# A local-attention layer on one Trainium2 core: SiLU as x times (1 + tanh(x/2)), with the product on VectorE

## What is computed

```python
def _L3_ffn_ref(x, ln_gamma, ln_beta, fc1_q, fc1_scales, fc1_bias, fc2_q, fc2_scales, fc2_bias):
    residual = x
    h = (x - mu) * rsqrt(var + EPS) * ln_gamma + ln_beta      # 8 x 512 tokens of 256
    w1 = _dequant(fc1_q, fc1_scales, G)                       # 256 x 1024
    y = hf @ w1 + fc1_bias
    y = jax.nn.silu(y)                                        # 4096 x 1024
    w2 = _dequant(fc2_q, fc2_scales, G)                       # 1024 x 256
    z = y @ w2 + fc2_bias
    return residual + 0.5 * z.reshape(residual.shape)
```

## Time and profile before

| what | value |
|---|---|
| time, median of 3 runs (lowest, highest) | 3257.53 us (3250.82, 3258.21) |
| the profiled execution | 3265.37 us, span 3263.7 us |
| TensorE busy | 2919.4 us, 89% of the span |
| VectorE busy | 1855.6 us, 57% |
| ScalarE busy | 1379.5 us, 42% |
| GpSimd busy | 327.3 us, 10% |
| layer L3's loop, one pass of seven | 88.67 us |

### The profile page before, as it was taken

One profiled execution on the slowest core, in us unless ns is written; L12 is line 12 of the kernel. 1 busy time (PEld: TensorE's weight loads), 2 busy tenths in 40 slices (PEclk: granted clock), 3 DMA queues, 4 the chain that ended last, 5 costly groups with the idle time before them and its releaser, 6 DMA issues.

```text
span 3263.7 us, 50711 instructions
## 1 busy us (share of the span) xinstructions
PE 2919.4 (89%) x14374; PEld 1828.7 (56%) x14407; DVE 1855.6 (57%) x4470; ACT 1379.5 (42%) x1993; POOL 327.3 (10%) x353
## 2 busy tenths in 40 slices
PE   5999999999989888888789989999997798888888
PEld 3455545554544444444357767766664466666666
DVE  5656665666547777777646666652223555444442
ACT  1544454445425555554454554433232333333333
POOL 0000000000000000000211121121112211111110
PEclk7999999999878999999999999999998899999999
DMA  6433543254122121212230110132211433333340
GB/s 207 138 103 85 162 138 106 81 162 138 55 72 63 57 66 59 63 61 66 76 139 32 51 45 32 45 112 84 86 61 55 123 82 65 91 91 92 78 89 17
DMA packets 144299, 279.77 MB, mean 86 GB/s; under 512 B 22384, under 2 KB 80113, under 8 KB 134161
## 3 DMA queue, kind: packets, MB, share of 16 engines
q1 hardware_dynamic: 131760, 244.90, 26.1%
q0 software_dynamic: 10464, 28.59, 3.1%
q10 hardware_dynamic: 2016, 5.58, 0.5%
HBM read 179.31 MB, written 99.68 MB: 85 GB/s over the span
## 4 chain that ended last, share of the span: by engine, by line
PE 74%; DVE 9%; issue 5%; ACT 4%; DMA 4%; another core or an unknown queue 1%; SPq 1%; DVEq 0%; POOL 0%; ACTq 0%; POOLq 0%
PE bank_u L559 6%; PE pair L599 5%; PE pair L543 5%; PE pair L700 4%; PE pair L1984 4%; PE bank L2426 3%; PE bank L488 3%; DVE nmax L870 3%; PE pair L2883 3%; PE bank_m L2847 3%; PE pair L744 3%; PE bank L2847 3%; PE bank L520 2%; PE pair L499 2%; PE pair L1406 2%
## 5 line engine op out<-in xcount | busy, mean ns | idle before, releaser
L776 ACT ACTIVATE probs<-pair 128x1024 f32<-128x1024 f32 x512 | 501.2, 1020 | 220.2 <-PE pair L543 219.1
L870 DVE TENSOR_REDUCE nmax<-bank 128x1 f32<-128x512 f32 x664 | 442.2, 686 | 210.6 <-PE bank L520 147.8
L870 DVE TENSOR_REDUCE nmax<-bank_m 128x1 f32<-128x512 f32 x360 | 246.7, 685 | 114.5 <-PE bank_m L520 67.6
L559 PE MATMUL bank_u<-probs,vext 128*32 128x512 f32 x2048 | 294.0, 648 | 0.6 <-ACT uraw L763 0.5
L520 PE MATMUL bank<-k_a,q_a 96*128 96x512 f32 x336 | 173.6, 551 | 24.1 <-DMA k_a<-parts_dram 20.6
L543 PE MATMUL pair<-q_a,k_a 98*128 98x512 f32 x512 | 172.6, 444 | 17.1 <-ACT probs L776 11.8
L2019 ACT ACTIVATE probs<-pair 128x896 f32<-128x896 f32 x128 | 115.8, 918 | 131.1 <-PE pair L1906 78.1
L2116 DVE CUSTOM_DVE_ANT_0 bank<-bank,mask_q 128x128 f32<-128x128 f32 (+1 forms) x320 | 118.6, 416 | 80.1 <-PE bank L1888 73.1
L543 PEld LDWEIGHTS pair<-q_a,k_a 98*128 98x128 f32 x512 | 89.2, 199 | 112.5 <-ACT probs L776 65.3
L1379 PE MATMUL bank<-k,q 62*128 62x512 f32 x302 | 115.2, 485 | 26.7 <-DVE nmax L870 26.7
L1984 PE MATMUL pair<-fc,hid 128*128 128x256 f32 x512 | 131.2, 382 | 6.0 <-ACT probs L2019 6.0
(11 more groups left out here) (422 smaller groups left out, 5946.2 us busy)
## 6 DMA issues: line engine op xcount, KB each, us to landing
parts_dram<-parts SPq DMA_DIRECT2D x64, 512.0 KB, 2.8
q_a<-parts_dram SPq DMA_DIRECT2D x31, 512.0 KB, 5.3
k_a<-parts_dram SPq DMA_DIRECT2D x31, 512.0 KB, 7.2
q<-parts_dram SPq DMA_DIRECT2D x97, 128.0 KB, 2.6
xs<-xres SPq DMA_DIRECT2D x24, 512.0 KB, 3.0
xl<-xs SPq DMA_DIRECT2D x24, 512.0 KB, 3.9
x_in<-xg SPq DMA_DIRECT2D x74, 128.0 KB, 2.1
yg_dram<-y_out POOLq DMA_DIRECT2D x72, 128.0 KB, 2.0
```

What stands on the lines that cost most here:

```text
L559: ins = nc.tensor.matmul(bank_u[32 * h:32 * h + 32, :], vext[:, kt, kv(g, h), :], probs[:, kt % 2, h * SEQ:(h + 1) * SEQ], start=(kt == 0) ...
L776: nc.scalar.activation(probs[:, kt % 2, hp * 2 * SEQ:hp * 2 * SEQ + n], st.tile(l, name)[:, 0:n], ACT.Exp).then_inc(st.free["act"].sem, 1)
L870: nc.vector.tensor_reduce(nmax[:, g % 2, qt, h:h + 1], sc.tile(l, name)[:], AX, ALU.max, negate=True).then_inc(sc.free["dve"].sem, 1)
```

## The change

SiLU(y) = y sigmoid(y) = (y / 2) (1 + tanh(y / 2)). ScalarE now writes tanh((h + b)/2) into a new tile `gate3` (one tile for all eight, with the bias halved in `half_b`), then h + b into `hid3[:, i, :]` by Identity, which hands the PSUM bank back. VectorE multiplies: `hid3 = (gate3 + 1) * hid3`. The factor 1/2 goes into `fc2`, which was scaled by 0.5 and is scaled by 0.25 now. A new signal `hid_ready` counts the products: ScalarE's tanh of tile i waits for the product of tile i - 1, since that reads `gate3`, and TensorE's output matmuls wait for all eight. On VectorE product 0 stands ahead of group 3's first maxima, 1 behind two of them, 2 ahead of the fifth and sixth, 3 ahead of the last two, and 4 to 7 in a row behind the splits.

```diff
@@ dve_setup3
-                nc.vector.tensor_scalar(fc2[:], fc2[:], 0.5, None, ALU.mult).then_inc(dve_set3, 1)
+                nc.vector.tensor_scalar(fc2[:], fc2[:], 0.25, None, ALU.mult).then_inc(dve_set3, 1)
+                nc.vector.tensor_scalar(half_b[:], fc1_b[:], 0.5, None, ALU.mult).then_inc(dve_set3, 1)
@@ pe3
-                pe.wait_ge(*done(sc, l, it, ("H", 7)))
+                pe.wait_ge(*hid_ready.at(l, it, 8))
@@ act3
             def hidden(i):
                 act.wait_ge(*sc.filled(l, it, ("H", i)))
-                nc.scalar.activation(hid3[:, i, :], sc.tile(l, ("H", i))[:], ACT.Silu,
+                act.wait_ge(*hid_ready.at(l, it, i))
+                nc.scalar.activation(gate3[:], sc.tile(l, ("H", i))[:], ACT.Tanh, bias=half_b[:, i:i + 1], scale=0.5)
+                nc.scalar.activation(hid3[:, i, :], sc.tile(l, ("H", i))[:], ACT.Identity,
                                      bias=fc1_b[:, i:i + 1]).then_inc(sc.free["act"].sem, 1)
@@ dve3
+            def hidden(first, last):
+                for i in range(first, last):
+                    dve.wait_ge(*done(sc, l, it, ("H", i)))
+                    nc.vector.scalar_tensor_tensor(hid3[:, i, :], gate3[:], 1.0, hid3[:, i, :], ALU.add, ALU.mult)\
+                      .then_inc(hid_ready.sem, 1)
@@ dve3, the order of the back part
             if back:
-                maxima(3, 0, 4)
+                hidden(0, 1)
+                maxima(3, 0, 2)
+                hidden(1, 2)
+                maxima(3, 2, 4)
@@
             if back:
-                maxima(3, 4, 8)
+                hidden(2, 3)
+                maxima(3, 4, 6)
+                hidden(3, 4)
+                maxima(3, 6, 8)
                 dve_normalise_heads(dve, l, it, step, 0)
@@
+            if back:
+                hidden(4, 8)
             if front:
                 dve.wait_ge(*rstd3_ready.at(l, it, 1))
```

More of the change, by code:

```diff
@@ L1803, in build @@
         fc1_b = sb("fc1_b", [P, 8], F32, l3)
+        half_b = sb("half_b", [P, 8], F32, l3)
+        gate3 = sb("gate3", [P, SEQ], F32, l3)
         hn = sb("hn", [P, TT, DIM], F32, l3)
@@ L1827, in build @@
         rstd3_ready = sig("rstd3_ready", [0, 0, 0, (1, 0)], "gpsimd")
+        hid_ready = sig("hid_ready", [0, 0, 0, (0, 8)], "vector")
         hn_ready = sig("hn_ready", [0, 0, 0, (TT, 0)], "vector")
@@ L1847, in dve_setup3 @@
             elif c == 9:
-                nc.vector.tensor_scalar(fc2[:], fc2[:], 0.5, None, ALU.mult).then_inc(dve_set3, 1)
+                nc.vector.tensor_scalar(fc2[:], fc2[:], 0.25, None, ALU.mult).then_inc(dve_set3, 1)
+                nc.vector.tensor_scalar(half_b[:], fc1_b[:], 0.5, None, ALU.mult).then_inc(dve_set3, 1)
             elif c == 10:
-                dve.wait_ge(dve_set3, 10)
+                dve.wait_ge(dve_set3, 11)
                 flat = fc2[:, :, :].rearrange("p k n -> p (k n)")
@@ L3068, in _ @@
                     act_blocks(act, it)
-            act.wait_ge(dve_set3, 12)
+            act.wait_ge(dve_set3, 13)
             act3(act, PRE3, 0, step)
@@ L3157, in _ @@
                 pe.wait_ge(*free.at(PRE3, 0))
-            pe.wait_ge(dve_set3, 12)
+            pe.wait_ge(dve_set3, 13)
             pe.wait_ge(pool_set3, 2)
```

## The result

The changed kernel takes 3297.1 us (median of 4 runs, 3292.2 to 3298.1) beside 3257.9 us for the kernel before (4 runs). The ratio is 1.0113, 95% interval 1.0097 to 1.013: 32 to 42 us slower (39.2 by the medians), where 28.7 was forecast. 3297.1 us lies inside the stated range of 3264 to 3298 us, 1 us from its upper end, and above the 3276 to 3294 us of the likeliest case alone. The profiled execution took 3292.2 us, its span is 3290.5.

What follows compares the result with a forecast made beforehand. TensorE, busy 89% of the span, was taken as the bound. Removed loads counted 0; the longer chain, 7 x 3.46 + 4.48 = 28.7 us on the 3257.5 us median, gave 3286 us, range 3264 to 3298.

Steps and rivals of the forecast that it cites:

- the likeliest case: The longer chain through H0 to H3 in the fourth layer sets the time: 3276 to 3294 us, chance 0.73.
- slower still: VectorE's products 4 to 7 each wait 1.88 us beside GpSimd's indirect DMAs: about 3294 to 3298 us, chance 0.04.
- What is removed: two table loads a batch: 16 ScalarE table loads around SiLU go, 1.283 us each; booked at 0, since other waits follow them.
- The pause belongs to the table load: The pause ahead of group 2's first exponential goes with the load: 3225 us, faster, chance 0.12.
- The loads' own time was on the path: Removing 16 loads of 1.28 us gives 20.5 us back: 3266 us, chance 0.03.
- What is added: Per hidden tile: ScalarE's pair takes 1.27 us where SiLU took 0.69, VectorE's product 0.76 us, plus two new waits.
- The chain through H0 to H3: Banks come back later and maxima queue behind products, so Q0 on TensorE starts 3.46 us later a batch.
- The last batch: The same chain from H0 to the seventh maxima tile grows from 9.11 to 13.59 us: +4.48 us.
- H4 to H7 hide: The slower tiles H4 to H7 cost nothing; the pause covers them with 6.5 us, and without it they hide too.
- Sum: 7 x 3.46 + 4.48 = 28.7 us slower over the fourth layer, bounds 25 to 33 us.
- The pause: ScalarE's 6.99 us unexplained wait ahead of group 2's first exponential stays, still 5 to 7 us after the change.
- swallow the shift: If the pause's end hangs on an unmoved transfer, seven shifts of 3.46 fit into it: 3262 us, chance 0.08.

Runs made afterwards that it cites:

- the first experiment: The tanh alone: the kernel before with tanh in place of SiLU, no table loads between, nothing added; 3242.2 beside 3241.3 us, ratio 1.0000.
- experiment 3: The changed kernel with ScalarE's tanh and Identity pair but without VectorE's 8 products and the waits on them; ratio 1.0047 to the kernel before.
- Experiment 8: Both edits on the changed kernel: Identity hands the bank back before tanh, and products in VectorE's gap with three gate buffers; ratio 0.9868 to the kernel before.
- experiment 6: The changed kernel with the pair turned round: Identity reads the bank and hands it back, tanh then reads SBUF; ratio 0.9950 to the kernel before.
- experiment 2: The product alone: the changed kernel with SiLU and its table loads back, VectorE's 8 instructions and their waits kept; ratio 1.0034 to the kernel before.
- experiment 4: The kernel before with GpSimd's indirect gather held until group 3's first scores are in their bank; ratio 0.9985 to the kernel before.
- the paced gather: The kernel before with a small GpSimd copy behind each of a batch's first three indirect gathers; 3188.3 beside 3189.2 us, ratio 0.9995.
- experiment 7: The changed kernel with three gate buffers and the products of H0 to H3 moved off the maxima's way on VectorE; ratio 0.9906 to the kernel before.
- experiments 10 and 12: Gather held until the batch's last stack loads landed, in the kernel before (3208.7 us, 1.0056) and with both edits (3213.4 us, 1.0068).
- the second comparison of the change: The changed kernel unaltered, timed again beside the kernel before on the chip where its parts were timed; 3286.7 beside 3243.2 us, ratio 1.0141.

## Why the prediction was right, and what it left out

The direction and the chain were right. That the time lies in the stated range is partly luck: the likeliest case with its own bounds, 25 to 33 us, would have ended at 3294, and 3297.1 is inside only because the range had been widened up for the rival "slower still". What that rival describes did not happen. The products of H4 to H7 start 0.03 us behind their Identity beside the gather, and H4 to H7 takes 6.1 us, no longer than the 6.3 (3 x 2.11) of the forecast. The excess came from terms that the sum had at nothing, below. The near hit on the profiled execution, 3292.2 us for 3294.1, is luck too: the layers ahead were 9.1 us shorter in it.

**What is removed: two table loads a batch.** Booked at 0, measured 0 with 4 us either side. "The pause belongs to the table load" and "The loads' own time was on the path" both fall with the first experiment. The Trainium skill (ScalarE: Activation LUTs, What ACT_TABLE_LOAD costs) has 2.66 us for a switch, draining included. Here a load of 1.28 is followed by 0.58 us of waiting for TensorE, so that the whole switch, from SiLU's end to the exponential's start, takes 1.88 us, and leaving it out moves the exponential by nothing. The measurement decides against pricing these 16 by that figure.

**What is added.** Forecast 1.27 us for the pair and 0.76 for the product; the rows have 1.27 (0.59 to the second start, then 0.68) and 0.69.

**The chain through H0 to H3.** 3.46 us a batch forecast. From H0's start to the copy of Q0's bank it is 16.43 in place of 13.02, +3.41. Only its inner split was wrong: the waits ahead of H2 and Q0 are 0.77 and 0.49 us, not "near 2" and "0.8 to 1", since part of the delay stands as 0.43 ahead of the transposes at L529 and 0.32 ahead of those at L723. The price of the pair inside the chain was misjudged in the expectation of experiment 3 (0.6 to 1.2 us a batch, measured 1.96), but not in the forecast of the whole. Experiment 8 bears the chain out from the other side: with the bank back early and the products out of the maxima's way 0.34 us a batch are left of it, though ScalarE and VectorE do as much as in the change.

**The last batch.** +4.48 forecast, +4.2 in the profile.

**H4 to H7 hide.** Right in mechanism: from H4 to group 2's first exponential it takes 14.83 us in the mean of the second to seventh batch after and 14.75 before. In the first batch the pause stood elsewhere after the change, one step later, between the first exponentials of groups 2 and 3 (9.50 us for 8.24).

**Sum.** The size fell short here. 28.7 us forecast; 7 x 3.41 + 4.2 = 28.1 read from the profile. The comparison says 37 (39.2 by the medians), and the layer as a whole is 35.9 us longer in the pair of profiles (the layers ahead of it were 9.1 us shorter in that execution, which the change doesn't touch; over all profiles they vary from 2539 to 2561 us). The missing 8 us are small additions that the sum had at nothing. H4 to the next batch is +5.0 over seven batches: +2.0 in the first, where the gather starts later, and in the others mostly behind the pause, where the stretch to group 3's exponential varies between 5.5 and 6.7 us in either kernel. Up to H0 it is +0.9, from Q0 to H4 +0.5, and 1.7 us are one clock row:

```profile
3139.66:3143.34 3.68, 3.68 (x6) 1.66 (x7) 1.94 (x8) 0.00 (x0) 0.00 (x0) 0.54 0.04 9
```

This is H2 of the seventh batch in the changed kernel by windows: a granted clock of 0.54 (1.2 GHz for nearly all of it), and 3.68 us in which the same four matmuls and two small ones fit into about 2 us elsewhere. Such a row came once in the first profile of the change, twice in the second (there also in the last batch, 80.1 us for 78.4), three times in experiment 6, and once in experiment 2; not in the layer's chain in the kernel before. TensorE's waits ahead of it (0.97, 0.27, 0.43 and 0.78 us) were within 0.01 us the same as in the batch before, where the clock stayed up, so what sets it off stays open.

**The pause** stays with the change, as forecast, and does not swallow the shift. That it follows the gather is shown by experiment 4, and that is why the shift came through in full: the gather starts behind the stores of the splits, and those are late by the chain. Its price is 8.4 us a batch (328.5 us for seven batches in the kernel before, 269.8 with the paced gather): 6.5 ahead of group 2's first exponential and 1.8 in the stretch to group 3's, where the clock is at its lower level behind the pause and at 1.00 without it. The prediction had 1.7 for that second part. What decides whether it is there at all is open: in experiments 6 to 8 the 19 batches with a drawn-out start of the gather had no pause ahead of group 2's exponential and the two others had one (in experiment 7 one step later, between the exponentials of groups 2 and 3), while the product alone drew out only the third gather in its second to seventh batch (1.30 us) and kept the pause there. A drawn-out first gather alone is not enough: it took 1.32 us in the first batch of the change, which has the pause one step later. Nor were late signals gone in the 19. In many of them a wait of 1 to 3 us is put down to remote or issue further on, and in the first batch with both edits VectorE has one of 5.12 us (at 2594.64); H7 to the next batch is 280.8 us with both edits, and 269.8 with the paced gather, which has no such wait of 0.9 us or more. And none of this was tested against a kernel before that had the pause. So it is not shown that the edits, and not the chance of the loading, took the pause away. It is also open whether the version with both edits ever beats the kernel before. It was 45 us faster beside one with the pause. At 3198 us it is not faster than the 3189 us that the kernel before takes without it, though these two were not run side by side; in experiments 10 and 12, which were, both with the gather held back, it is 4.7 us behind. Of the second comparison of the change, 43 us by the medians, the profiled execution places all but the 7 us by which it lies under the median.

## What to carry to other kernels

When one activation is split into two that read the same PSUM bank, the cost is the time for which the bank is held longer, once for each consumer of the ring; let the first one read the bank, hand it back, and work on from SBUF. An instruction added on another engine belongs into that engine's gap, found in the timeline, and not in front of the work that hands banks back. A table load whose place is already a wait for another engine is worth nothing, and, before a gain or loss is credited to an edit, look whether a pause that comes and goes between loadings of the same code is in both profiles.

## What the runs showed of the hardware

- The same kernel was at 3243 and at 3189 us on the same chip in two comparisons, each steady within 13 us. The difference of 54 us is seven times 7.7, near the pause of a batch: H7 to the next batch is 45.6 to 48.1 us in the kernel before with it (328.5 for seven) and 324.6 for seven in the tanh alone, and with the paced gather, without it, 38.5 (269.8 for seven). That the kernel before lost its pause at 3189 us is read from its time; it was not profiled there.
- Beside indirect gathers at a pitch of 1.25 us TensorE's signals can arrive 3 to 7 us late, with no instruction to blame (H7 to the exponential 5.9 to 9.7 us in the kernel before, 2.56 without the pause); without the table loads it is the same (6.7 to 8.2 us).
- A product of VectorE with two operands in SBUF that begins 0.1 to 0.3 us ahead of an indirect DMA draws its issue out, the first of a batch from 1.10 to 1.36 us, the next two from 0.96 to 1.27 and 1.40. One that begins with it or during it does not (1.10 and 0.95 to 0.96 us in the change). By the Trainium skill (GPSIMD Engine Reference, Key points) GpSimd shares its SBUF interfaces with VectorE, which contends when it reads two inputs from SBUF; the rows agree for a product that begins ahead of the issue.
- TensorE's clock can fall to its lower level for a single tile (0.54 granted over 3.68 us) after waits no longer than in the batches beside it.
